# Another order in tiles 1 and 2 of a cross-attention and mixture kernel: the output projection of tile 0, the context maxima and the last weight halves stand later

## The reference, cut to what matters

```python
# layer 1: the context is the weight of a matmul, both sides rounded to fp8 steps per block
xq = quant_dequant_act_1x128(layernorm(x));  wq = quant_dequant_weight_128x128(ctx)   # 128x128 blocks of ctx
x  = x + einsum('emk,enk->emn', xq, wq)                    # e = batch
# layer 2: router, 8 basis units of width 256, one down projection, and a shared unit
xt = layernorm(x).reshape(T, 512)
probs = softmax(xt @ w_router);  topk_p, topk_idx = top_k(probs, 4);  topk_w = topk_p / (sum(topk_p) + EPS)
basis = silu((xt @ w_gate).reshape(T, 8, 256)) * (xt @ w_up).reshape(T, 8, 256)
mix_sel = mix[topk_idx]                                    # mix: normalised squared amplitudes, 128 experts x 8
out = sum over the 4 picks of coeff * ((mix_sel . basis) @ w_down)
out = out + silu(xt @ shared_w_gate) * (xt @ shared_w_up) @ shared_w_down
return x + out
```

## Time and profile before

| | us |
|---|---|
| median of three runs | 602.69 (599.99 to 602.70) |
| profiled execution, its own time | 602.66 |
| its span, first to last instruction | 600.9 |

### The profile page before, as it was taken

The page is one execution under the profiler, slowest core; times in us unless marked ns, Lnnn a source line. Parts: engine busy times, 40 slices in busy tenths (PEclk is TensorE's granted clock), DMA queues, the critical chain, the costliest instruction groups (busy, mean ns, idle before and its releaser), DMA issues.

```text
span 600.9 us, 7839 instructions
## 1 busy us (share of the span) xinstructions
PE 538.7 (90%) x2571; PEld 252.6 (42%) x2586; DVE 391.8 (65%) x1122; ACT 238.9 (40%) x339; POOL 203.9 (34%) x242
## 2 busy tenths in 40 slices
PE   0359977799799999999999999999999999999983
PEld 0124433344344444444544444444444444444431
DVE  6977888966866676858475777756665748463211
ACT  4677885232524242342433332343334343323110
POOL 2431040384613135544414134725223141402020
PEclk9999999899999999999999999999999999999997
DMA  8624521111022312112123121121211202020101
GB/s 295 247 87 140 176 88 26 36 28 45 17 54 45 113 36 54 36 30 59 26 54 107 26 63 27 37 52 36 46 42 37 52 27 63 9 53 11 44 0 45
DMA packets 61753, 37.10 MB, mean 62 GB/s; under 512 B 49168, under 2 KB 49680, under 8 KB 61712
## 3 DMA queue, kind: packets, MB, share of 16 engines
q1 hardware_dynamic: 61712, 36.59, 22.3%
HBM read 20.72 MB, written 4.19 MB: 41 GB/s over the span
## 4 chain that ended last, share of the span: by engine, by line
PE 70%; DVE 9%; issue 5%; ACT 2%; POOL 1%; DMA 0%; POOLq 0%; DVEq 0%; SPq 0%; ACTq 0%
PE gate L970 28%; PE up L970 28%; PE even L1000 9%; DVE x L1182 2%; PE odd L952 2%; DVE gate_up L1345 2%; PE odd L892 1%; DVE part L1274 1%; ACT L688 1%; DVE down_lo L1345 1%; DVE ctx_m L1104 1%; DMA hT_hi<-hs_hi 0%; DVE hid L1266 0%; PE up L923 0%; PE turn L867 0%
## 5 line engine op out<-in xcount | busy, mean ns | idle before, releaser
L970 PE MATMUL up<-gate_up,zT_hi 128*128 128x512 f16 x600 | 178.7, 380 | 0.7
L970 PE MATMUL gate<-gate_up,zT_hi 128*128 128x512 f16 x600 | 179.3, 381 | 0.0
L704 ACT ACTIVATE silu<-gate,w_back 128x512 f32<-128x512 f32 x75 | 51.6, 688 | 180.0 <-PE gate L970 179.8
L970 PE MATMUL gate<-gate_up,zT_lo 128*128 128x512 f16 x300 | 114.1, 380 | 0.0
L970 PE MATMUL up<-gate_up,zT_lo 128*128 128x512 f16 x300 | 114.0, 380 | 0.0
L1274 DVE SCALAR_TENSOR_TENSOR part<-up,coef,silu 128x256 f32<-128x256 f32 x128 | 55.9, 478 | 52.8 <-PE up L970 51.0
L559 POOL TENSOR_TENSOR hid<-hid,part 128x256 f32<-128x256 f32 x48 | 34.8, 724 | 155.5 <-DVE part L1274 155.4
L970 PEld LDWEIGHTS gate<-gate_up,zT_hi 128*128 128x128 f16 x600 | 58.8, 100 | 66.5 <-issue 1.6
L970 PEld LDWEIGHTS up<-gate_up,zT_hi 128*128 128x128 f16 x600 | 57.9, 98 | 62.4
L543 POOL TENSOR_TENSOR gain<-var,minus_half 128x1 f32<-128x1 f32 x16 | 9.2, 576 | 133.5 <-DVE neg_mean L1196 133.5
L970 PEld LDWEIGHTS gate<-gate_up,zT_lo 128*128 128x128 f16 x300 | 29.4, 98 | 35.7 <-issue 0.6
(11 more groups left out here) (176 smaller groups left out, 799.6 us busy)
## 6 DMA issues: line engine op xcount, KB each, us to landing
ctx_in<-in_ctx SPq DMA_DIRECT2D x16, 256.0 KB, 3.4
x_in<-in_x SPq DMA_DIRECT2D x16, 256.0 KB, 2.9
out<-y_out SPq DMA_DIRECT2D x16, 256.0 KB, 2.2
stage<-in_L_ffn_w_gate SPq DMA_DIRECT2D x2, 1024.0 KB, 7.5
stage<-in_L_ffn_w_up SPq DMA_DIRECT2D x2, 1024.0 KB, 5.0
stage<-in_L_ffn_shared_w_gate SPq DMA_DIRECT2D x1, 1024.0 KB, 7.8
stage<-in_L_ffn_shared_w_up SPq DMA_DIRECT2D x1, 1024.0 KB, 8.8
ctx_qT<-in_L_ffn_w_up SPq DMA_DIRECT2D x1, 1024.0 KB, 12.1
```

What stands on the lines that cost most here:

```text
L704: nc.scalar.activation(silu[:, k % 2, :], gate_ps[k % 2][:], ACT.Silu, scale=w_back[:, n:n + 1] if t else 1.0 / LN_GAIN).then_inc(silu_don ...
L970: mm = nc.tensor.matmul(ps[:], zT[a][:, t % 2, kc, :], wgu[:, n - 1 + i, w, kc, :], start=(m == 0), stop=(m == 3 * KC - 1))
```

## The change

- TensorE: `down(0)` moves from after `pair(1, 0)` to after `pair(1, 3)`. `flip_ctx(1)` moves from pair 1 to pair 3 of tile 1, `spread_ctx(1)` from its first to its sixth quarter. In tile 2 the four `turn_ctx` stand later. In all tiles `turn_weight(t)` moves from pair 3 of the tile before to the middle of `pair(t, -1)`, and `coefs(t)` from the start of that pair to the start of `pair(t, 0)`.
- VectorE: in tile 1 `lo_w(DOWN)`, `lo_w(9)`, `lo_w(10)`, the maxima and `lane_ctx(1)` stand later, and `combine(1, 1)` ahead of the maxima; `finish(0)` moves into tile 2. In all tiles `coefficients(t)` stands after the statistics.
- ScalarE: `split_w(DOWN)` moves into tile 1; the scaling of batch 1's context (16 instructions of 128x128) comes here from GpSimd (4 of 128x512); `keep_weight(t)` follows the silu of the shared unit; in tile 2 the `keep_ctx` stand later.
- SyncE: `store(0)` moves from tile 1 to tile 2, behind `turn_h(1)`.

```diff
-    ORDER = list(range(9)) + [DOWN, 9, 10]
+    ORDER = list(range(DOWN)) + [DOWN]
 # SyncE
                 if t >= 1:
                     turn_h(t - 1)
+                if t == 2:
+                    store(0)
+                if t >= 2:
                     store(t - 1)
 # GpSimd, tile 1
-                if t == 1:
-                    for c in range(NB, 2 * NB):
-                        scale_ctx(c)
 # ScalarE
-            def scale_ctx(k):
-                act.wait_ge(ctx_lane, CTX_LANE)
+            def scale_ctx(c):
+                k = c % NB
+                act.wait_ge(ctx_lane, CTX_LANE * (c // NB + 1))
...
                 silus(t, -1)
+                keep_weight(t)
                 h_hi(t - 1)
...
                 silus(t, 1)
+                if t == 1:
+                    split_w(DOWN)
+                for c in early[:1]:
+                    keep_ctx(c)
...
                 if front:
                     exps(t + 1)
+                if t == 1:
+                    scale_ctx(NB)
+                    scale_ctx(NB + 1)
+                if t == 2:
+                    keep_ctx(late[0])
                 silus(t, 3)
-                if front:
-                    keep_weight(t + 1)
+                if t == 2:
+                    keep_ctx(late[1])
+                if t == 1:
+                    scale_ctx(NB + 2)
+                    scale_ctx(NB + 3)
 # TensorE, the loop over t
+                shared = {4: lambda: turn_weight(t)}
...
+                pair(t, -1, shared)
+                zero = {0: lambda: coefs(t)}
...
+                pair(t, 0, zero)
+                if t > 1:
+                    down(s)
...
-                elif t == 1:
-                    pair(t, 1, {6: lambda: flip_ctx(1)})
...
-                third = {6: lambda: turn_weight(u)} if front else {}
+                third = {}
                 if t == 1:
-                    third[0] = lambda: spread_ctx(1)
+                    third[1] = lambda: flip_ctx(1)
+                    third[5] = lambda: spread_ctx(1)
...
+                elif early:
+                    second[3] = lambda: turn_ctx(early[1])
+                    third[1] = lambda: turn_ctx(late[0])
+                    third[6] = lambda: turn_ctx(late[1])
...
                 pair(t, 3, third)
+                if t == 1:
+                    down(s)
```

More of the change, by code:

```diff
@@ L763, in _ @@
             split_w(8)
-            keep_weight(1)
             silus(0, 3)
-            split_w(DOWN)
             for t in range(1, TILES):
@@ L780, in _ @@
                 abs_shared(t)
-                for c in early:
-                    keep_ctx(c)
                 if front:
@@ L790, in _ @@
                 silus(t, 1)
+                if t == 1:
+                    split_w(DOWN)
+                for c in early[:1]:
+                    keep_ctx(c)
                 for c in late[:1]:
-                    if t % NB == 1 or t == 2:
+                    if t % NB == 1:
                         keep_ctx(c)
@@ L797, in _ @@
                 silus(t, 2)
+                for c in early[1:]:
+                    keep_ctx(c)
                 for c in late[1:]:
-                    if t % NB == 1 or t == 2:
+                    if t % NB == 1:
                         keep_ctx(c)
@@ L1026, in _ @@
             spread_w(5)
-            turn_weight(1)
             for t in range(1, TILES):
@@ L1032, in _ @@
                 early, late = ctx_turns(t)
+                shared = {4: lambda: turn_weight(t)}
                 if t == 1:
[L1034 to L1040, removed]
+                    shared[2] = lambda: turn_x(2)
+                if front:
+                    shared[6] = lambda: attend(u, 0)
+                    shared[7] = lambda: attend(u, 1)
+                pair(t, -1, shared)
+                zero = {0: lambda: coefs(t)}
+                if front:
+                    zero[2] = lambda: attend(u, 2)
+                    zero[6] = lambda: attend(u, 3)
+                pair(t, 0, zero)
+                if t > 1:
+                    down(s)
                 if early:
-                    pair(t, 1, {1: lambda: turn_ctx(early[0]), 5: lambda: turn_ctx(early[1])})
-                elif t == 1:
-                    pair(t, 1, {6: lambda: flip_ctx(1)})
+                    pair(t, 1, {5: lambda: turn_ctx(early[0])})
                 elif late and t % NB == 2:
@@ L1113, in mask_ctx @@
                     dve.wait_ge(ctx_scaled_dve, c + 1)
-                elif c < NB:
+                elif c < 2 * NB:
                     dve.wait_ge(ctx_scaled_act, c - 1)
                 else:
-                    dve.wait_ge(ctx_scaled_pool, c - NB + 1)
+                    dve.wait_ge(ctx_scaled_pool, c - 2 * NB + 1)
                 if c >= 2:
@@ L1439, in _ @@
                     mask_ctx(c)
-                coefficients(t)
+                if t == 2:
+                    finish(0)
                 hid_chain = scale_h(s)
@@ L1444, in _ @@
                 split_h(hid_chain, s)
-                if t == 1:
-                    lo_w(DOWN)
                 if front:
@@ L1449, in _ @@
                 combine(t, -1)
-                if t == 1:
-                    lo_w(9)
                 if b > 0:
@@ L1457, in _ @@
                     stats2(u)
+                if t == 1:
+                    lo_w(9)
                 if ahead:
                     stats(t + 2)
+                coefficients(t)
                 combine(t, 0)
-                if t == 1:
-                    lo_w(10)
-                finish(s)
+                if t > 1:
+                    finish(s)
                 if front:
@@ L1466, in _ @@
                 if t == 1:
+                    lo_w(10)
+                    combine(1, 1)
                     for c in range(NB, 2 * NB):
@@ L1478, in _ @@
                         max_ctx((b + 1) * NB + k)
-                combine(t, 1)
+                if t > 1:
+                    combine(t, 1)
                 if front:
@@ L1482, in _ @@
                 if t == 1:
+                    ctx_chain = lane_ctx(1)
+                    lo_w(DOWN)
                     scales_ctx(ctx_chain, 1)
```

2 lines of the change are left out of this document (removed).

## The result

The changed kernel took 594.83 us (median of four runs, 594.26 to 595.55), the kernel before on the same chips 602.03 (599.99 to 602.70). The ratio is 0.9885, with a 95% interval of 0.9861 to 0.9909. The forecast was 592.0, with 588.5 to 597.0.

A forecast was written before the change was run, and what follows sets the result against it. The prediction took VectorE to set the pace in tile 1 and TensorE from tile 3 on. 602.66 - 6.4 (tiles 1 and 2) - 4.4 (later turned weights) = 591.9, say 592.0 us, range 588.5 to 597.0.

The forecast's parts named there:

- the forecast's own case: Whole kernel: the expected gains come about, giving a time from 590 to 594 us; chance 0.46.
- rival 2: Tile 1, GpSimd: lo_w(10) starts ahead of tile 3's reciprocal root and holds it, +2.1 us, or 594.0; chance 0.13.
- tile 3's first gate: Sign in the new trace: TensorE's first gate of tile 3 comes at 158 to 162.
- tiles 4 and 5: Sign in the new trace: these tiles together take some 64.1 us; still 66 us would show the forecast wrong.
- VectorE's list decides when `down(0)` can start.: Tile 1: VectorE's reordered list, ending with lo_w(DOWN) at 122.3, sets the start of down(0).
- I add 2.0 us: Tile 1: VectorE held up by GpSimd, as the two exclude each other; 2.0 us, ends 0 and 4.1.
- the 26.27 without any hold: Tile 1: length in us of VectorE's new list from the first attention piece of tile 2 through lo_w(DOWN), if nothing holds it.
- A new wait of 1.2 us for `finish(0)`.: Tile 2: attend(3, 0) on TensorE waits for finish(0) on VectorE to free bank "even"; 1.2 us, ends 0 and 2.5.
- Turned weights, 4.4 us.: Tiles 4, 5, 8 and 9: turning weights later hides TensorE's waits for them, twice 2.2 us; ends 0 and 4.4.
- It moves along: Tiles 4, 5, 8 and 9: VectorE's attention, late next, itself waits for TensorE's attend and so shifts with it.
- The clock (rival 1).: End of tile 1: the granted clock falls again during down(0) or after, costing up to 1.7 us, 593 to 593.7; chance 0.17.
- Sum.: Whole kernel: 602.66 less 6.4 up to tile 3 and 4.4 for turned weights gives 591.9, say 592.0 us.

The follow-up runs named there:

- the first experiment: The changed kernel with GpSimd's reciprocal root for tile 3 moved ahead of the first sum of parts in tile 1: 592.75 us, ratio 0.9848.
- both mends: The changed kernel with the root ahead of the parts, finish(0) directly behind the last combine and two context masks behind tile 2's shared combine: 591.07 us, ratio 0.9812.

## Why the prediction held, point by point

The time lies inside the range from 588.5 to 597.0, but above the forecast's own case, 590 to 594. The part that it missed is for the most part rival 2, which the forecast had priced at 594.0 and given 0.13; that the total lies only 0.8 us above that price is in part luck, since two more misses, of 0.9 and 0.7 us, are partly offset by 0.65 us at the end that the sum did not have (last point). Of its signs, tile 3's first gate came at 162.99, not at 158 to 162, and tiles 4 and 5 took 258.66 - 194.55 = 64.1 us from first gate to first gate, as said.

- *VectorE's list decides when `down(0)` can start.* Held: it started at 124.57, within 0.05 us of the end of `down_lo` (121.12 + 3.40 = 124.52), and what shortened the list shortened the time.
- *"I add 2.0 us" for the exclusion with GpSimd.* This term of the sum was mis-sized, and in the way of rival 2, which had 0.13. The list from 93.94 to the start of its next instruction at 124.44 took 30.5 us, 4.2 more than the 26.27 without any hold: 2.58 for the silu, 0.48 in `lo_w(10)`, 1.05 in the top four. The holds that the step names came to 1.5 us (none at `z_lo(2)`); the 2.58 it did not have. It took it that `lo_w(10)` would wait for the root; but a sum of parts stood ahead of the root and `lo_w(10)` was waiting when that ended. Rival 2 priced it at 2.1, and the first experiment measured 2.1. The rule of the Trainium skill (SBUF — State Buffer, section Who interferes with whom) that whoever is first keeps the port for the whole instruction agrees with all three rows: the sum kept `lo_w(10)` waiting, and that the root. In the changed kernel and in the experiments with the finish, the maxima and the scaling moved, the waiting `lo_w(10)` was issued ahead of the root and went first (106.30 and 106.93 in the changed kernel; the root held 2.59 to 2.60 us). In the run with the weights back in place the root was issued first (105.80 and 106.31) and came through in 1.00 us; so half a microsecond decides it.
- *A new wait of 1.2 us for `finish(0)`.* Right in place and cause, 2.12 in size, inside its ends. Masks and finish took 128.83 to 134.30, 5.5 us, where the sum had 5.2. Beside GpSimd's parts and roundings three of the four mask instructions took 0.83 to 1.37 us, the first, with none beside it at its start, 0.42, and the finish's first step, one number per row, 1.22.
- *Turned weights, 4.4 us.* Right in cause; 3.68 from `down(2)` to `down(9)`, since `down` then waits 0.4 us longer for attention in tiles 6 and 10. "It moves along" was nearly, not fully true.
- *The clock (rival 1).* It did not fall in tiles 1 and 2 in the profile of the changed kernel, and did in those of six of its seven edits, after the same wait of 3.4 us (4.1 in one). The seventh, with the low half of DOWN ahead of the top four, has no wait so long there. Where TensorE was to wait for the finish anyway, part of it cost nothing, as the forecast said: with the root moved and with the maxima first that wait was 1.28 us in place of 2.12.
- *Sum.* 602.66 - 3.45 - 3.68 - 0.65 = 594.9, which is the profiled execution's own time (594.92), against the sum's 591.9. Of the 3.0 us between, 2.1 are the root, 0.9 the wait for the finish and 0.7 the turned weights; the 0.65 at the end, which the sum did not have, goes the other way.

## What to carry to other kernels

Where several waits lie close together, find the engine whose list has no pause and sum that list in its new order; taking waits out of another engine's list is worth only what it shortens there. Where two engines exclude each other, a tiny instruction behind a long one on the other engine can cost the long one's whole length (here 2.59 us in place of 0.54), so place the tiny one ahead or give its waiter something to do. And a part of a change that brings nothing by itself can be what lets another part pay.

## What the hardware showed that was not expected

The granted clock is not a property of the order alone. With the same wait of 3.39 us ahead of `spread_ctx(1)` it stayed at 1.00 in the changed kernel's profile and was at its lower level from 121 to 127 with the finish moved. In tile 0, where the order is the same in all of them, it fell between 82 and 88 us in the profiles of five edits (the maxima, the finish, both mends, the last low half, the scaling) and not in that of the changed kernel. The four executions of the changed kernel had mean granted clocks of 0.985 to 0.994. So one profile of a kernel does not say what the clock did in its other executions.

Runs of one kernel differ by 0.6 to 5.6 us. With the last low half ahead of the top four the clock goes with that: three executions at a mean clock of 0.994 took 589.2 to 589.8 us, three at 0.988 took 591.1 to 592.1. In the changed kernel it does not (594.92 at 0.994, 594.26 at 0.991), so it is not the only cause.
